# One semaphore and no waits between the indirect DMAs that scatter the routing order

## The reference, cut to what matters

```python
xn = _layernorm(x, axis=-1)
# attention
q, k, v = xn @ Wq.T + bq, xn @ Wk.T + bk, xn @ Wv.T + bv
scores = where(mask, einsum("bqhd,bkhd->bhqk", q, k) * SCALE, -10000.0)
ctx = einsum("bhqk,bkhd->bqhd", softmax(scores) + 1e-9, v)
attn = ctx @ Wo.T + bo
# experts
logits = xt @ gate_w.T
_, idx = top_k(logits + beta, 2)
probs = sigmoid(take_along_axis(logits, idx, axis=-1))
combined = sum over the two chosen e of probs_e * (silu(xt @ gate_e) * (xt @ up_e)) @ down_e
return x + attn + combined + shared_out
```

## Time and profile before

| | |
|---|---|
| median of 3 runs | 1853.15 us (1845.76 to 1856.8) |
| the profiled execution's own time | 1853.15 us |
| its span, first to last instruction | 1851.4 us |
| mean granted TensorE clock | 0.937 |
| busy: PE, PEld, DVE, ACT, POOL | 88%, 71%, 61%, 52%, 52% |
| DMA indirect L362 (order_d) | 128 instructions, 124.2 us busy, 185.1 us idle ahead of them |

### The profile page before, as it was taken

One profiled execution on the slowest core, in us unless ns is written; L12 is line 12 of the kernel. 1 busy time (PEld: TensorE's weight loads), 2 busy tenths in 40 slices (PEclk: granted clock), 3 DMA queues, 4 the chain that ended last, 5 costly groups with the idle time before them and its releaser, 6 DMA issues.

```text
span 1851.4 us, 39076 instructions
## 1 busy us (share of the span) xinstructions
PE 1635.2 (88%) x11313; PEld 1323.5 (71%) x11313; DVE 1129.1 (61%) x3793; ACT 962.3 (52%) x1914; POOL 963.7 (52%) x915
## 2 busy tenths in 40 slices
PE   5987870899999999999999789899888988899987
PEld 4765750788888888888888656667666666666665
DVE  5877870466656656566665656666665666666652
ACT  4544530454544545445454356666666666666563
POOL 1343446312222121221211168888888888888887
PEclk9988995899999999999999679999999999999999
DMA  5766672444444444444455466666666666676642
GB/s 161 238 208 234 232 279 73 160 145 151 154 137 157 147 152 151 141 155 142 152 156 115 92 145 160 155 151 143 148 146 150 147 156 154 159 161 157 149 126 78
DMA packets 219824, 287.89 MB, mean 156 GB/s; under 512 B 67193, under 2 KB 133882, under 8 KB 219642
## 3 DMA queue, kind: packets, MB, share of 16 engines
q1 hardware_dynamic: 169802, 201.80, 39.1%
q0 software_dynamic: 17728, 38.30, 8.2%
q10 hardware_dynamic: 32240, 47.20, 7.9%
HBM read 194.92 MB, written 82.31 MB: 150 GB/s over the span
## 4 chain that ended last, share of the span: by engine, by line
PE 63%; DVE 11%; issue 9%; ACT 6%; POOL 4%; ACTq 4%; DMA 2%; DVEq 1%; another core or an unknown queue 0%; POOLq 0%; SPq 0%
PE psum L149 33%; PE psum L759 13%; PE psum L1217 5%; PE psum L1257 5%; PE psum L1240 3%; ACT plain_arena L1371 2%; PE psum L852 2%; POOL order_d L362 2%; DVE split_arena L632 1%; ACTq L1390 1%; ACTq L1391 1%; ACT plain_arena L1385 1%; DVE plain_arena L1495 1%; PE psum L1228 1%; ACT plain_arena L1403 1%
## 5 line engine op out<-in xcount | busy, mean ns | idle before, releaser
L149 PE MATMUL psum<-split_arena 128*128 128x512 f32 (+2 forms) x4560 | 1019.7, 374 | 67.0 <-DVE plain_arena L1495 55.0
L149 PEld LDWEIGHTS psum<-split_arena 128*128 128x128 f32 x4560 | 785.5, 199 | 223.6 <-DVE plain_arena L1495 57.4
L1480 DVE CUSTOM_DVE_ANT_0 plain_arena<-psum,mask 128x256 f32<-128x256 f32 (+1 forms) x1024 | 338.4, 385 | 217.0 <-PE psum L1217 203.7
L834 POOL DMA_INDIRECT plain_arena<-xn_d,c_ix x156 | 152.3, 976 | 521.3 <-PE psum L852 464.6
L1371 ACT ACTIVATE plain_arena<-psum 128x512 f32<-128x512 f32 (+1 forms) x512 | 250.9, 542 | 250.4 <-PE psum L1240 225.3
L759 PE MATMUL psum<-split_arena 128*128 128x256 f32 x1872 | 233.8, 285 | 0.0
L759 PEld LDWEIGHTS psum<-split_arena 128*128 128x128 f32 x1872 | 226.9, 192 | 0.1
L362 POOL DMA_INDIRECT order_d<-plain_arena,slot x128 | 124.2, 970 | 185.1 <-DMA order_d<-plain_arena,slot 113.0
L898 ACT ACTIVATE plain_arena<-psum 128x512 f32<-128x512 f32 x156 | 93.5, 599 | 218.1 <-PE psum L149 211.5
L924 DVE TENSOR_TENSOR split_arena<-plain_arena,split_arena 128x1024 fp32r<-128x1024 f32 x117 | 143.0, 1224 | 66.0 <-ACT split_arena L879 65.7
L1217 PE MATMUL psum<-split_arena 48*128 48x256 f32 (+1 forms) x1024 | 157.7, 355 | 12.4 <-POOL plain_arena L1203 6.5
(11 more groups left out here) (146 smaller groups left out, 1718.8 us busy)
## 6 DMA issues: line engine op xcount, KB each, us to landing
plain_arena<-in_gate_w SPq DMA_DIRECT2D x39, 512.0 KB, 3.3
plain_arena<-in_up_w SPq DMA_DIRECT2D x39, 512.0 KB, 3.3
plain_arena<-in_down_w SPq DMA_DIRECT2D x39, 512.0 KB
y_d<-plain_arena ACTq DMA_DIRECT2D x39, 512.0 KB, 2.7
plain_arena<-in_x SPq DMA_DIRECT2D x32, 512.0 KB, 7.5
q_d<-split_arena SPq DMA_DIRECT2D x32, 512.0 KB
k_d<-split_arena SPq DMA_DIRECT2D x32, 512.0 KB
split_arena<-q_d SPq DMA_DIRECT2D x128, 128.0 KB, 3.6
```

The costliest lines, as they stand in the source:

```text
L149: last = pe.matmul(out, lhs_t(p), rhs(q), start=(begins and c == 0 and k == 0), stop=(ends and c == len(chunks) - 1 and k == 2), skip_grou ...
L834: pool.indirect_dma_start(c_x[:, a, :], None, xn_d, bass.IndirectOffsetOnAxis(c_ix[:, u, a, 0:1], 0)).then_inc(c_ldx, 16)
L1480: last = dve.tensor_tensor_reduce(b_junk[:, 2 * par + i % 2, 0:cols], psum[:, par, at:at + cols], mask[:, 2 * P - cols:2 * P], -1.0, 3e38, ...
```

## The change

The two semaphores of the scatters become one. POOL's wait ahead of each scatter is taken out, so that after the wait for a batch's `p_at` its 8 scatters are issued one behind the other. SP waits for the one semaphore at the count of all 128 scatters (32 x 4 x 16 = 2048, where each of the two counted 16 x 4 x 16 = 1024). Nothing else is altered: the same 128 scatters, in the same order, with the same data.

```diff
@@ -242,7 +242,7 @@
         p_at = sem("p_slots_known")
-        p_sc = [sem(f"p_order_scattered{c}") for c in range(2)]
+        p_sc = sem("p_order_scattered")
@@ -357,11 +357,9 @@
                 pool.wait_ge(p_at, b + 1)
                 for a in range(T):
                     for c in range(2):
-                        if b * T + a >= 1:
-                            pool.wait_ge(p_sc[c], 16 * (b * T + a))
                         pool.indirect_dma_start(
                             order_d, bass.IndirectOffsetOnAxis(slot[:, b * T + a, c:c + 1], 0),
-                            token[:, b * T + a, :], None).then_inc(p_sc[c], 16)
+                            token[:, b * T + a, :], None).then_inc(p_sc, 16)
@@ -802,8 +800,7 @@
             weights(0, None)
-            for c in range(2):
-                sp.wait_ge(p_sc[c], 16 * T * B)
+            sp.wait_ge(p_sc, 32 * T * B)
             for u in range(2):
                 order(u, u)
```

## The result

The changed kernel takes 1871.74 us (median of 8 runs, 1863.27 to 1877.68), the kernel before 1850.49 us (8 runs, 1845.54 to 1858.32). The ratio is 1.0109, with a 95% interval from 1.0079 to 1.0139: 21 us slower, where the prediction had 36.7 us faster. The profiled execution took 1876.68 us, with a span of 1874.9 us, 23.5 us more than before.

What follows compares the result with a forecast made beforehand. The prediction took the scatters, delayed by POOL's landing waits, to set the projection stage's end while PE stood idle. PE starting at 291.5 instead of 328.23 saves 36.7 us: 1853.15 - 36.7 = 1816.5 us, range 1806 to 1832.

Steps and rivals of the forecast that it cites:

- The waits' removal in the loop: Projection loop: removing POOL's landing waits saves nothing by itself, as no engine waits for a scatter before L806.
- The scatters' traffic: DMA queue 0 in the loop: share rises from 1.9% to 2.6%, costed at nothing, at most 1.5 us.
- SP's arrival at its wait for the scatters: End of the projection stage: SP reaches L806 at 277.3 in any case, behind key stores and weight loads.
- Loss of clock: Rival for the expert stage: shorter PE rest lowers its clock; at 0.93 it costs 51 us, 1868 us; chance 0.04.
- the last 16 scatters follow without a break: Tail of the projection stage: POOL keeps up until the last batches, last scatter starting at 276.0 instead of 314.97.
- The last landing: Behind the last scatter: it lands beside weight loads, so SP goes on at 280.0, bounds 277.6 and 282.1.
- SP's wait 0 to 5 us: SP at L806, waiting for the scatters: 0 to 5 us instead of 39.8.
- The list's load behind the weights: SP's queue: the list loads behind 1.5 MB of weights and lands at 282.2, bounds 281.7 and 283.8.
- From the list to PE: Gathers before the expert stage: 9.35 us taken unchanged, so PE starts at 291.5, bounds 289.3 and 293.2.
- PE's wait of about 20 us instead of 56.6: Start of the expert stage: PE's wait ahead of its first gathered transposes shrinks to about 20 us.
- Rival A: Scatter issue: two scatters under way already suffice, so nothing is gained and the time is 1853 us; chance 0.03.
- rival B: DMA queue 0: the backlog moves there from POOL, so only 16 us are saved, 1837 us; chance 0.06.

Runs made afterwards that it cites:

- e8: The kernel before, unaltered, run for its trace in a session of the second kind: 1864.7 us in its one run.
- e6: The changed kernel unaltered, in a session of the second kind: 1883.33 us, 1.0117 of the kernel before.
- e13: The changed kernel unaltered, as a control in a session of the second kind: 1874.3 us, 1.0125 of the kernel before.
- e7: The changed kernel with its two semaphores back, without landing waits, second kind of session: 1889.89 us, 1.0161 of the kernel before.
- e9: The changed kernel with all scatters held until the last batch's slots are known, second kind of session: 1959.28 us, 1.0570 of before.
- e10: The changed kernel with a 128x256-word memset between a batch's scatters, second kind of session: 1829.43 us, 0.9865 of before.
- e14: The changed kernel with scatters held to the end and eight 128x1024 memsets per batch in the loop: 1978.03 us, 1.0674 of before.
- e15: The changed kernel with scatters held to the end and eight plain DMAs per batch in the loop: 1969.88 us, 1.0646 of before.
- e18: The changed kernel unaltered, as a control in a session of the first kind: 1795.89 us, 0.9766 of the kernel before.
- e3: The changed kernel with all scatters held until the last batch's slots are known, first kind of session: 1941.9 us, 1.0579 of before.
- e1: The changed kernel with its two semaphores back, without landing waits, first kind of session: 1797.68 us, 0.9801 of before.
- e4: The changed kernel with a 128x256-word memset between a batch's scatters, first kind of session: 1799.8 us, 0.9813 of before.
- e5: The changed kernel with four semaphores, each scatter waiting for the one four before, first kind of session: 1797.46 us, 0.9796 of before.
- e12: The changed kernel with a 128x512-word memset between a batch's scatters, second kind of session: 1829.73 us, 0.9883 of before.
- e16: The changed kernel with 128x512-word memsets between scatters in the first 14 batches only, first kind of session: 1804.43 us, 0.9824 of before.

## Why the prediction was wrong

**The step that failed** is the cost of the burst in the loop: "*The waits' removal in the loop* saves nothing by itself: POOL has no other work there, and no engine waits for a scatter before L806", and with it "*The scatters' traffic* costs little ... I cost it at nothing", with 1.5 us as its upper bound. In the measurement the last slots moved from 262.05 to 314.12, 52.07 us, and with them the key stores and SP's arrival at its wait for the scatters, which the prediction held fixed at 277.3 (the first weight load is issued at 329.25). Nobody waits for a scatter in the loop, that was right. But I asked only who waits for the scatters' results, and not what their issue does to the others.

The trace of before held a sign of it, and the prediction passed it over. Its landing waits mostly broke the rows of scatters up: up to 255 us only two rows of five stand 1.27 us apart, from 113.9 and from 183.2, and none is longer. Some 10 us behind the start of the first and 7 us behind that of the second, DVE waited for a result of PE with the mark "remote". First POOL and DVE around the first of them in order of time, then the two waits in the list of 48 to 255 us (total us, times, longest):

```profile
115.21 0.99 POOL L362 DMA_INDIRECT order_d<-plain_arena,slot  x1 [0.30 <-issue]
...
122.11 0.97 POOL L362 DMA_INDIRECT order_d<-plain_arena,slot  x1 [0.30 <-issue]
124.02 0.17 DVE L599 TENSOR_TENSOR plain_arena<-psum,plain_arena 128x8 f32<-128x8 f32 x1 [1.62 <-remote]
```

```profile
DVE plain_arena L599 <- remote: 2.8, 2, 1.6
```

The update of PE that ended the first wait stands 3.55 us behind the last matmul that could have made it, and of PE's 121 updates recorded from 48 to 260 us 8 more are over 0.5 us late (e8's trace of the same kernel has 4, up to 2.1 us). Small as 2.8 us is, it was a reason to give the denser burst a cost; I bounded it by DMA share alone.

**What is shown.** In sessions of the second kind unspaced scatters lengthen the ordinary turn from 14.1 to about 20 us (the result, e6, e13), with one semaphore or two (e7), and PE's signals come up to 5.4 us late in that loop; without scatters in the loop (e9), or with 0.2 us between them (e10), the turn is 14.1 or 15.1 us. Memsets of 8 us (e14) and plain DMAs of the same packets (e15) don't do it. In sessions of the first kind the same program has turns of 14.0 to 14.2 us (e18). So it takes both, the burst and the condition, and before the change the waits for landings did, unasked, most of what e10's memsets do. **What is open** is what the condition is. Chip 3 showed the first kind in two sessions and the second in one, so it isn't the chip. That a trace of the second kind lacks about a fifth of the records of semaphore updates (30,972 in e18, 24,002 in the result, one program), and that the fault is a late update, suggests that the two hang together; that is only argued. Lost records alone don't make late signals: e9 has 26,149 records where the same program in the first kind (e3) has 30,964, and none of PE's updates in its loop is late. No run tells what makes both. The Trainium skill's page "NOTIFIC — the notification-queue block", in the section on overflow and its three behaviours, says that the block that writes such records holds its sources back inside rather than lose one there; no run here shows that this happens.

**Loss of clock** was a rival (C), with its price right in kind and its place wrong. I put it at the expert stage, which stayed at 1.00, and it came in the projection loop, 0.77 from 60 to 260 us. It follows PE's stops (in the turn shown PE stands still from 188.06 and the clock falls at 190.7) and is not the first cause; how the 5.6 us of a turn divide between the stop and the half clock behind it I did not separate. The Trainium skill's page "TensorE: Matmul & The Clock Gate", in the section on how clock oscillation bites in real kernels, has this form: a loop with a long enough wait in every turn drops TensorE to the lower level each time. By that rule, the trace agrees: 0.50 over 10.1 us of a 19.7 us turn.

**The steps of the tail held**, counted from the last slots, in both traces.

- POOL keeps up and the last 16 scatters follow without a break. Forecast: the last starts 276.0 - 262.05 = 14 us behind the slots; it was 330.30 - 314.12 = 16.2 us, and in e18 269.55 - 252.87 = 16.7 us. What was missing in the 14 us is one gap behind the first of the 16 scatters, 2.98 us and in e18 3.63 us where 0.30 is usual. The earlier trace rows show it with 2.23 us; I had taken it for a part of the mean pace. It comes once, behind the 113th of the 128 scatters, in 18 of the 20 traces; why is open.
- The last landing: I took 4.0 us, between 2.1 and 4.9; it was 5.56 us, and 4.29 us in e18. The Trainium skill's page "DMA: Bandwidth & Descriptors", in the section on the anatomy of one DMA by the software path, would have given an estimate of 2.0 us for 8 KB; both measured landings are over twice that, beside the weight loads.
- SP's wait 0 to 5 us: 5.2 us, and 5.5 us in e18.
- The list's load behind the weights: 1.61 us, and 1.62 us in e18; the first weight load was issued at 329.25, 6.6 us ahead of the list, where in the trace of before the weights had moved within 5.7 us of its issue (275.88 to 281.6), so what I allowed for queueing was not needed.
- From the list to PE 9.35 us: 347.00 - 337.49 = 9.51 us, and 284.94 - 275.48 = 9.46 us in e18.

The chain of e18, from which its figures are:

```profile
269.55 4.29 DMA order_d<-plain_arena,slot
273.86 1.62 DMA c_ix<-order_d
...
282.08 2.72 DMA plain_arena<-xn_d,c_ix
284.94 1.95 PE psum L849 x8
```

- PE's wait of about 20 us instead of 56.6: 20.8 us, and 22.2 us in e18.

So the forecast of 36.7 us is near what the change gives where the loop isn't disturbed: e18 has 41 us, by medians of one session (0.9766; the forecast was 1816.5 / 1853.15 = 0.980). No trace of the kernel before was taken in a session of the first kind, so where those 41 us lie is not shown row by row. Rival A, nothing gained, is refuted by SP's wait of 5.2 us. So is rival B: the last scatter landed 5.6 us behind its start, with no pile of others.

**The best version** by these runs depends on the condition. In sessions of the first kind it is the changed kernel (0.977), and e1, e4 and e5 (0.980 to 0.981, in another session of that kind) can't be told from it. Over both kinds it is a spaced one: e4 and e10, one program, 0.981 and 0.987, and e12, 0.988 in the second kind, where the changed kernel is 1.012. Spacing in the loop alone (e16) gives 0.982 in the first kind; in the second it wasn't tried.

## What to carry to other kernels

A wait that no one needs for its data may still pace an engine. Before taking one out, ask what its engine will then do without a pause, and price that on every engine beside it, not only on those that wait for the result. And where a trace names no releaser for a wait, and a result of one engine reaches the next microseconds late, look at what a third engine issues in that time, and compare the time of the semaphore update with the end of the instruction that makes it; here a pause of 0.2 us between the third engine's instructions took most of the loss away. A short wait of this sort in the trace of before, 1.6 us here, is reason enough to look. If a kernel's control moves by 1% between sessions, rerun the changed kernel in both conditions before believing either verdict: here they are 0.977 and 1.012.

## What the hardware showed that was not expected

- While POOL issued indirect DMAs 1.27 us apart (0.97 us of issue and a gap of 0.30 us), the semaphore updates of TensorE for ScalarE came up to 5.7 us behind the matmuls' ends in one kind of session; 1.47 us apart removed most of the loss (the latest was 3.4 us late), and 1.7 us apart all of it (none over 0.02 us late in e12's loop).
- A plain DMA on the same engine is issued in 4.26 / 8 = 0.53 us, an indirect one of the same 128 rows of 64 bytes in 1.27 us.
- One GpSimd gap of 2.1 to 3.6 us came behind the 113th of 128 indirect scatters in 18 of 20 traces, at whatever pace they were issued.
- The kernel before takes 1836 to 1838 us in one kind of session and 1850 to 1859 us in the other, 1%, more than the intervals of most ratios here. From PE's start in the expert stage to the end, the medians of the traces of the two kinds differ by some 19 us, whatever the kernel.
